# GpSimd normalises the head outputs of a delta-rule attention stage; head weights folded into the projection, GpSimd's reset moved to the iteration's end

## The chip, the cores and the metric

The kernel runs on one core of a Trainium2 chip. The metric is the device time of one execution in microseconds (us), from the start of the program to its end. Besides its DMA queues the core has TensorE (PE; its weight loads are shown as PEld), VectorE (DVE), ScalarE (ACT), GpSimd (POOL) and SyncE (SP, which here only issues transfers). Each engine works through its own instructions in order; semaphores order them against each other.

## What is computed

Six blocks work on x of 64 x 64 tokens x 128 channels in float32, each added to x: self-attention, cross-attention, a routed feed-forward layer, a gated delta-rule attention with spiking gates, a gated cross-attention, and a second routed layer. The change lies in the fourth block alone:

```python
h = silu(conv(rms(x)));  q, k, v, drive = h @ Wq, h @ Wk, h @ Wv, h @ Wspike     # 8 heads of 64
alpha_base = silu(h @ Wau + bau) @ Wad + bad;  beta_base = h @ Wbeta + bbeta
# per time step (spike: the membrane 0.9 * mem + drive is over its threshold)
alpha = sigmoid(alpha_base + alpha_spike * spike)
beta  = sigmoid(beta_base + sum(spike * beta_spike, -1))
active = sum(spike) > 0                            # per head; inactive: alpha = 1, beta = 0
s = s * alpha;  s = s + (beta * k) * (v - k @ s);  out = q @ s
# after the steps
y = out * rsqrt(mean(out * out) + 1e-6) * head_norm_w
y = x + (y @ Wo) * sigmoid(gate);  z = rms(y) * ff_norm_w
y = y + (silu(z @ Wff1) * (z @ Wff3)) @ Wff2
```

## The kernel before

The block is the function `delta()`. The time recurrence is not stepped: for each group of 8 sequences (512 tokens, `T`) the triangular system of 64 steps is inverted by doubling. There are 8 groups (`NG`), and the loop over `it` from -2 to 8 is a software pipeline written out by hand on each engine. In iteration `it` the core work is that of group `it`, the front work (projections, norms, decays, beta) that of group `it + 1`, and the tail work (head norm, output projection, feed-forward) that of group `it - 1`. Heads go in four pairs, `hp` or `j` from 0 to 3. Iterations 1 to 6 have core, front and tail; iteration 0 has no tail, 7 no front, 8 only a tail.

The core work runs over stages. TensorE forms the products of a head pair (`diag`, L2231; `products(g, l)`, L2244) in two pairs of PSUM banks; VectorE takes them over into `AP` with `masked(g, stage, hp)` (L2708 for stage 0, L2719 for the rest) and multiplies k and q by the decays (`scale_first`, L2727; `scale`, L2742 and L2744); GpSimd multiplies `kr` and the decays in its own `scale` (L2630, L2631). The products of pair `hp` at a level may only overwrite a bank pair when the `masked` two before it is done (`pair_free`). `first_inverse` (VectorE L2750 and L2753, four pairs) builds the first inverse; `ax` and `xw` (L2259, L2268, L2290) double it level by level, ScalarE copying their PSUM banks out (`w_out` L2476, `x_out` L2482 and L2484). `ax(it, 1)` needs `first_inverse` and all of `masked(it, 2, ...)`. The first step of a core writes the negative identity into half of `AP`: `reset` on GpSimd (L2619), which waits until the last `ax` of the group before has read it.

The products of front and tail work go through two further PSUM banks (6 and 7) in turn, in an order given by the list `FILLS`: a fill may only start when what the fill two before it wrote has been read. For the change the order ..., k 0 to 3, cb, wo, q 0 to 3, al 0 to 3, ... counts: q 0 waits for the reading of cb, q 1 for that of wo.

The tail norm: ScalarE squares a head pair's output, TensorE sums (`t_ss`, L2178 and L2150), ScalarE makes Ln and Exp of it (`t_rms`, L2450 and L2452; the third and fourth wait until the first and second `o_normed` have read the double buffer), VectorE multiplies output, half the head weight and this reciprocal norm (`o_normed`, L2773, four times), TensorE projects (`t_wo`, L2188), VectorE multiplies by the gate (`t_gated`, L2782).

The count of spikes and the beta logits (`f_cb`): TensorE L2164 and L2166 in the bank of cb; ScalarE copies the logits (L2508); VectorE then turns the counts into 1e30 where a head had no spike, else 0 (L2839, rows 64 to 95 of `au`), which goes as an extra input row with a weight of one into the decays' product (`f_al`, L2138). Sigmoid of beta is ScalarE's `f_beta` (L2531), the masking by `active` VectorE's (L2844); the product `f_kr` (L2150) of TensorE needs it.

VectorE's order in an iteration: `masked(0)` with `scale_first`, four times; `o_normed` four times; `masked(1)` and `scale(0)` of pairs 0 and 1; `f_cb`; the same of pairs 2 and 3; `t_gated`; `first_inverse` four times; `masked(2)` and `scale(1)` four times; `t_y`; and on. Late in the iteration it advances the membrane of group `it + 2` in small steps on 128x32 elements (L2767, L2769), between which `f_beta`, `f_kr` and `t_out` stand. GpSimd's order: `reset`, `z_tok` (L2655), `scale(0)`, `squares` of k (L2648), `scale(1)`, `residual`, `scale(2)`, `squares` of q, `scale(3)`, `scale(4)`, and, after a wait for the end of the membrane, `spikes` (L2635).

## Time and profile before

| | us |
|---|---|
| median of 3 runs | 2898.83 (lowest 2896.13) |
| the profiled execution | 2903.73 |
| its span, first to last instruction | 2901.9 |
| `delta()` in the span | about 1095 to 2398 |
| one full iteration | about 156 to 160 |
| granted TensorE clock, mean over the span | 0.829 of full |
| busy: PE, DVE, ACT, POOL | 2361.8, 1634.3, 969.8, 732.5 |

One of the three runs took 7392.36 us; the median is not touched by it. A timeline row gives start, duration, engine, line, operation, output from input, count, and in brackets how long the engine was idle before it and what released it.

### The profile page before, as it was taken

The page shows a single profiled execution, that of the slowest core. Times are in us where ns is not written, and L with a number is a line of the kernel's source. Part 1 is how long each engine was busy: PE and PEld are TensorE (multiplying, and loading weights), DVE is VectorE, ACT ScalarE, POOL GpSimd, SP SyncE. Part 2 cuts the span into 40 slices and gives each one's busy share as a digit, 9 for nine tenths or more (in the row PEclk, how much of TensorE's full clock was granted, in tenths as well). Part 3 has the DMA queues.
Part 4 walks back from the last instruction along what each step waited for, and adds up shares of the span by engine and source line. Part 5 has one row for each costly group of instructions (what it writes and reads, how often), then busy time and mean ns, then how long its engine had stood idle before and what let it go on. Part 6 is the DMA issues. An engine that isn't in the chain of part 4 may idle for free. (4 is left out here: it accounts for less than half of the span.)

```text
span 2901.9 us, 74066 instructions
## 1 busy us (share of the span) xinstructions
PE 2361.8 (81%) x31128; PEld 1655.3 (57%) x31167; DVE 1634.3 (56%) x4406; ACT 969.8 (33%) x1910; POOL 732.5 (25%) x852
## 2 busy tenths in 40 slices
PE   7898989998778576888989898989988886956674
PEld 4666666666665332555656564656656755745553
DVE  4455555545362474767676676767564713477334
ACT  3343343434212253342424343333434331310222
POOL 0110101101016452424231314232241300112663
PEclk9799898979559786999999998999998975555776
DMA  4000000000021131000000000000000002000114
GB/s 150 9 1 9 9 9 5 1 1 1 7 74 44 47 135 47 3 21 6 21 6 21 6 3 24 3 20 6 2 6 2 7 1 90 2 30 19 44 44 113
DMA packets 42507, 75.80 MB, mean 26 GB/s; under 512 B 5989, under 2 KB 27245, under 8 KB 39621
## 3 DMA queue, kind: packets, MB, share of 16 engines
q1 hardware_dynamic: 35140, 56.63, 5.7%
q0 software_dynamic: 7040, 14.43, 1.8%
q8 instruction: 252, 4.13, 0.6%
q14 instruction: 75, 0.61, 0.1%
HBM read 46.73 MB, written 24.31 MB: 24 GB/s over the span
## 5 line engine op out<-in xcount | busy, mean ns | idle before, releaser
L2630 POOL TENSOR_TENSOR delta_scaled_beta_k<-delta_scaled_beta_k,delta_decays 128x256 f32<-128x256 f32 x160 | 122.1, 763 | 434.0 <-DVE weights_sb L2742 225.2
L2719 DVE COPY_PREDICATED delta_neg_a_and_p_t<-delta_level_int,bank 128x256 f32<-128x256 uint8 x384 | 179.2, 537 | 74.1 <-PE bank L2244 73.2
L2244 PE MATMUL bank<-weights_sb,delta_scaled_beta_k 64*64 64x64 f32 x6144 | 136.1, 234 | 85.6 <-DVE delta_neg_a_and_p_t L2719 79.2
L2268 PEld LDWEIGHTS bank<-delta_inverse,delta_neg_a_and_p_t 64*64 64x64 f32 x5120 | 176.8, 145 | 46.2 <-issue 45.8
L2268 PE MATMUL bank<-delta_inverse,delta_neg_a_and_p_t 64*64 64x64 f32 x5120 | 199.7, 232 | 0.0
L2244 PEld LDWEIGHTS bank<-weights_sb,delta_scaled_beta_k 64*64 64x64 f32 x6144 | 116.0, 145 | 122.6 <-DVE delta_neg_a_and_p_t L2719 98.1
L683 POOL TENSOR_TENSOR attn_probs<-attn_probs,attn_row_sum 128x512 f32<-128x512 f32 x64 | 65.4, 1043 | 397.7 <-DVE attn_row_sum L766 397.7
L2476 ACT ACTIVATE delta_two_less_ax<-bank 128x512 f32<-128x512 f32 x160 | 94.8, 597 | 208.6 <-PE bank L2268 208.4
L303 PE MATMUL bank<-attn_z_self_t,weights_sb 128*128 128x256 f32 x512 | 153.4, 452 | 13.3 <-DVE attn_cross_values L741 9.6
L312 PE MATMUL bank<-attn_w_value_out,attn_z_self_t 128*64 128x512 f32 x512 | 143.0, 684 | 2.1 <-DVE attn_z_value_out L706 1.4
L2150 PE MATMUL bank<-delta_head_rows,norm_sel 16*128 16x512 f32 x192 | 117.6, 712 | 27.2 <-DVE delta_head_rows L2844 19.8
L2290 PE MATMUL bank<-delta_two_less_ax,delta_inverse_t 64*64 64x64 f32 x4096 | 133.9, 219 | 2.4 <-issue 2.3
L750 DVE TENSOR_REDUCE attn_row_max<-bank 128x8 f32<-128x512 f32 x128 | 82.5, 686 | 90.9 <-PE bank L392 61.3
L303 PEld LDWEIGHTS bank<-attn_z_self_t,weights_sb 128*128 128x128 f32 x512 | 107.7, 223 | 45.1 <-issue 20.4
L2290 PEld LDWEIGHTS bank<-delta_two_less_ax,delta_inverse_t 64*64 64x64 f32 x4096 | 127.6, 136 | 3.5 <-issue 3.5
L2482 ACT ACTIVATE delta_inverse<-bank 128x512 f32<-128x512 f32 x128 | 76.4, 597 | 134.8 <-PE bank L2290 134.8
L574 ACT ACTIVATE attn_z_value_out<-bank 128x512 f32<-128x512 f32 x96 | 57.0, 594 | 166.1 <-PE bank L312 166.1
L2648 POOL TENSOR_TENSOR delta_kq_squared<-weights_sb 128x512 f32<-128x512 f32 x64 | 73.5, 1179 | 121.3 <-PE bank L2145 113.2
L2744 DVE TENSOR_TENSOR weights_sb<-weights_sb,delta_decays 128x512 f32<-128x512 f32 x128 | 97.9, 765 | 0.0
L2465 ACT ACTIVATE weights_sb<-bank 128x512 f32<-128x512 f32 x64 | 38.1, 597 | 178.2 <-PE bank L2131 178.2
L1392 POOL DMA_INDIRECT moe_z_sorted<-z_rows,moe_take_row x71 | 69.0, 971 | 112.7 <-DVE moe_take_row L1684 91.3
L1543 ACT ACTIVATE moe_hidden<-moe_pre_gelu 128x256 f32<-128x256 f32 x71 | 29.6, 417 | 198.2 <-DVE moe_pre_gelu L1705 121.1
(535 smaller groups left out, 5325.8 us busy)
## 6 DMA issues: line engine op xcount, KB each, us to landing
delta_drives<-front_drive SPq DMA_DIRECT2D x7, 1024.0 KB, 3.9
weights_sb<-in_w_moe_dram SPq DMA_DIRECT2D x1, 4352.0 KB, 14.7
z_rows<-moe_z_all SPq DMA_DIRECT2D x16, 256.0 KB, 2.3
delta_odd_spikes<-delta_drives SPq DMA_DIRECT2D x4, 1024.0 KB, 5.0
weights_sb<-moe_outs SPq DMA_DIRECT2D x8, 512.0 KB, 7.2
weights_sb<-delta_drives SPq DMA_DIRECT2D x3, 1024.0 KB, 5.1
weights_sb<-in_w_delta_dram SPq DMA_DIRECT2D x1, 2816.0 KB, 9.8
weights_sb<-in_ctx_tok_dram SPq DMA_DIRECT2D x8, 264.0 KB, 5.9
```

The lines of the kernel that those rows point to most:

```text
L303: last = pe.matmul(out_[:, i * 256:(i + 1) * 256], wA[:, 0 if kind == "q" else 1, m * 128:(m + 1) * 128], zA[:, g % 2, :], start=True, sto ...
L312: last = pe.matmul(out_[64 * hh:64 * hh + 64, :], zA[:, g % 2, 64 * b:64 * b + 64], vo[:, hh, 512 * half:512 * half + 512], start=True, st ...
L750: dve.tensor_reduce(mx[:, o % 2, h, :], ps[h], AX, ALU.max).then_inc(s["max"], 1)
L2150: return pe.matmul(out_[:, :], nsel[r, j, :], hrows[r, :], start=start, stop=True)
L2244: last = pe.matmul(two[eo][rows(sg), b4 * 64:b4 * 64 + 64], kr[r, hp, t], second(kq[r, g % 2, :, hp, t], c), start=b < 2, stop=True, skip_ ...
L2268: last = pe.matmul(out_[rows(sg), u], AP[rows(sg), hp, eo, b4, 0, :], X[rows(sg), hp, u], start=False, stop=True, skip_group_check=True)
L2290: last = pe.matmul(out_[rows(sg), u], lhsT, rhs, start=b == 0, stop=True, skip_group_check=True)
L2476: act.activation(W[:, hp, :], bank[4 + hp % 2][:, :], ACT.Copy).then_inc(s["w"], 1)
L2482: act.activation(X[:, hp, :], bank[4 + hp % 2][:, :], ACT.Copy).then_inc(s["x"], 1)
L2630: pool.tensor_tensor(r_[:, :, 0, :], r_[:, :, 0, :], a_[:, :, 1, 0:1].to_broadcast([128, T // (2 * c), c]), ALU.mult)
L2719: last = dve.copy_predicated(second(AP[:, hp, eo, :, :, :].rearrange("p b i n -> p (b i) n"), c), m_, PAIR[hp % 2][eo][:, :].rearrange("p ...
L2744: dve.tensor_tensor(v, v, f.unsqueeze(1).to_broadcast([128, 2, m, c]), ALU.mult).then_inc(s["scaled_kq"], 1)
```

## The change

VectorE's `o_normed` goes to GpSimd as a plain product of two tensors, at the start of GpSimd's iteration; the half head weight is multiplied once into the four blocks of the output projection's weights. VectorE's `f_cb` goes to ScalarE as Relu(1 - count), right behind the copy of the logits; the 1e30 goes into the weight row. GpSimd's `reset` and `z_tok` go from the start of an iteration to the end of the one before, ahead of `spikes`. ScalarE's `f_beta` goes ahead of `w_out(it, 5)`. On VectorE `first_inverse` goes ahead of `t_gated`.

```diff
@@ ScalarE, f_cb(g)
                         act.activation(hrows[BETA, :], J[at_fill["cb", g, 0] % 2][96:128, :], ACT.Copy).then_inc(s["logit"], 1)
+                        if g >= 1:
+                            act.wait_ge(s["al_ps"], nth_of("al", g - 1, 3))
+                            act.wait_ge(s["beta"], g)
+                        act.activation(au[64:96, :], J[at_fill["cb", g, 0] % 2][64:96, :], ACT.Relu, bias=ones[64:96, :], scale=-1.0)\
+                            .then_inc(s["cb_rd"], 1)
@@ ScalarE, iteration
                         act.preload_act_table(ACT.Sigmoid)
+                        if front:
+                            f_beta(it + 1)
                         if core:
                             w_out(it, 5)
                         if front:
-                            f_beta(it + 1)
                             f_alpha(it + 1)
@@ GpSimd
+                    def o_normed(g, j):
+                        pool.wait_ge(s["o_rstd"], HDP * g + j + 1)
+                        pool.tensor_tensor(oT[:, j, :], oT[:, j, :], orstd[:, j % 2, :], ALU.mult).then_inc(s["o_normed"], 1)
@@ GpSimd, iteration
-                        if core:
-                            reset(it)
                         if tail:
-                            z_tok(it - 1)
+                            for j in range(HDP):
+                                o_normed(it - 1, j)
                         if core:
                             scale(it, 0)
...
                             scale(it, 3)
                             scale(it, 4)
+                        if front:
+                            reset(it + 1)
+                        if core:
+                            z_tok(it)
                             if it + 2 < NG:
                                 spikes(it + 2)
@@ VectorE
-                    def o_normed(g, j):
-                        dve.wait_ge(s["o_rstd"], HDP * g + j + 1)
-                        dve.scalar_tensor_tensor(oT[:, j, :], oT[:, j, :], half_w[:, j:j + 1], orstd[:, j % 2, :], ALU.mult, ALU.mult)\
-                            .then_inc(s["o_normed"], 1)
...
-                    def f_cb(g):
-                        dve.wait_ge(s["logit"], g + 1)
-                        if g >= 1:
-                            dve.wait_ge(s["al_ps"], nth_of("al", g - 1, 3))
-                        dve.tensor_scalar(au[64:96, :], J[at_fill["cb", g, 0] % 2][64:96, :], 0.0, 1e30, ALU.is_equal, ALU.mult)\
-                            .then_inc(s["cb_rd"], 1)
-
                     def f_beta(g):
                         dve.wait_ge(s["sigmoid"], g + 1)
+                        dve.wait_ge(s["cb_rd"], g + 1)
@@ VectorE, once
-                    dve.tensor_scalar(half_w[:, :], col("headw", 0, HDP), 0.5, None, ALU.mult)
+                    link(dve.tensor_scalar(half_w[:, :], col("headw", 0, HDP), 0.5, None, ALU.mult))
+                    for n in range(HDP):
+                        w_ = wD[:, 7, n * 128:(n + 1) * 128]
+                        dve.tensor_scalar(w_, w_, half_w[:, n:n + 1], None, ALU.mult)
...
-                    dve.tensor_copy(wD[64:72, 4, :], nsel[0:8, 0:HDP, :].rearrange("p j d -> p (j d)"))
+                    dve.tensor_scalar(wD[64:72, 4, :], nsel[0:8, 0:HDP, :].rearrange("p j d -> p (j d)"), 1e30, None, ALU.mult)
+                    dve.memset(ones[:, :], 1.0)
@@ VectorE, iteration
-                        if tail:
-                            for j in range(HDP):
-                                o_normed(it - 1, j)
-                        if core:
-                            for hp in (0, 1):
+                        if core:
+                            for hp in range(HDP):
                                 masked(it, 1, hp)
                                 scale(it, 0, hp)
-                        if front:
-                            f_cb(it + 1)
-                        if core:
-                            for hp in (2, 3):
-                                masked(it, 1, hp)
-                                scale(it, 0, hp)
+                            for hp in range(HDP):
+                                first_inverse(it, hp)
                         if tail:
                             t_gated(it - 1)
                         if core:
-                            for hp in range(HDP):
-                                first_inverse(it, hp)
                             for hp in range(HDP):
                                 masked(it, 2, hp)
```

## Rows read from the trace of the kernel before

**Rows 1.** Busy time by stretch: length, PE, PEld, DVE, ACT, POOL, PEclk, DMA, GB/s
```profile
1100.00:2420.00 1320.00, 1133.09 (x21273) 749.80 (x21274) 832.64 (x2031) 472.88 (x797) 358.99 (x445) 0.90 0.04 14
```

**Rows 2.** Waits in 1105 to 2420: total us, times, longest us
```profile
DVE a_alpha_hidden_and_empty L2839 <- ACT delta_head_rows L2508: 68.3, 8, 10.5
```

**Rows 3.** Waits of PE in one full iteration, 1600 to 1757
```profile
PE bank L2244 <- DVE delta_neg_a_and_p_t L2719: 9.6, 4, 6.6
```

**Rows 4.** Timeline of the same iteration, 1611 to 1628
```profile
1611.36 1.41 DVE L2773 SCALAR_TENSOR_TENSOR delta_two_less_ax<-delta_two_less_ax,delta_half_head_norm,delta_o_rstd 128x512 f32<-128x512 f32 x2
...
1612.30 1.16 PE L2244 MATMUL bank<-weights_sb,delta_scaled_beta_k 64*64 64x64 f32 x64
...
1615.31 1.28 DVE L2719 COPY_PREDICATED delta_neg_a_and_p_t<-delta_level_int,bank 128x256 f32<-128x256 uint8 x2
...
1619.12 3.53 PE L2131 MATMUL bank<-group_conv_out,weights_sb 128*128 128x512 f32 x4
...
1627.13 3.84 PE L2188 MATMUL bank<-weights_sb,delta_two_less_ax 128*128 128x128 f32 x32
...
1627.86 0.69 DVE L2839 TENSOR_SCALAR a_alpha_hidden_and_empty<-bank 32x512 f32<-32x512 f32 x1 [8.64 <-ACT delta_head_rows L2508]
```

**Rows 5.** Timeline of the same iteration, 1632 to 1649
```profile
1632.34 1.98 PE L2131 MATMUL bank<-group_conv_out,weights_sb 128*128 128x512 f32 x4
...
1633.05 1.02 DVE L2750 TENSOR_TENSOR delta_inverse_t<-delta_neg_a_and_p_t,delta_two_eye 128x512 f32<-128x512 f32 x1
...
1639.65 1.26 DVE L2719 COPY_PREDICATED delta_neg_a_and_p_t<-delta_level_int,bank 128x256 f32<-128x256 uint8 x2
...
1640.96 1.13 PE L2244 MATMUL bank<-weights_sb,delta_scaled_beta_k 64*64 64x64 f32 x32 [6.64 <-DVE delta_neg_a_and_p_t L2719]
...
1643.77 3.15 PE L2131 MATMUL bank<-group_conv_out,weights_sb 128*128 128x512 f32 x4
...
1648.57 0.38 PE L2259 MATMUL bank<-delta_two_eye_bf,ident_bf 128*128 128x512 bf16 x1
```

**Rows 6.** Timeline of the same iteration, last inverse level, 1730 to 1735
```profile
1730.70 0.72 ACT L2531 ACTIVATE delta_head_rows<-delta_head_rows,delta_beta_bias 32x512 f32<-32x512 f32 x1
1731.44 2.56 ACT L2525 ACTIVATE delta_decays<-delta_decays,small_sb 128x512 f32<-128x512 f32 x4
...
1732.28 1.09 PE L2150 MATMUL bank<-delta_head_rows,norm_sel 16*128 16x512 f32 x2 [2.25 <-DVE delta_head_rows L2844]
...
1734.50 0.60 ACT L2484 ACTIVATE delta_inverse_t<-bank 128x512 f32<-128x512 f32 x1 [0.50 <-PE bank L2290]
```

**Rows 7.** Single lines: duration ns min/median/max, first and last start
```profile
L2648 POOL TENSOR_TENSOR delta_kq_squared<-weights_sb x64: 1034/1041/1486, 1108.3 to 2152.5; 128x512 f32<-128x512 f32 x64
L2619 POOL COPY delta_neg_a_and_p_t<-delta_neg_eye x8: 1887/1892/1893, 1128.0 to 2201.3; 128x2048 f32<-128x2048 f32 x8
L2655 POOL TENSOR_SCALAR weights_sb<-x_all,group_x_moments,group_x_rstd x32: 788/797/1226, 1289.7 to 2307.5; 128x128 f32<-128x128 f32 x32
L2742 DVE TENSOR_TENSOR weights_sb<-weights_sb,delta_decays x32: 716/946/1106, 1159.5 to 2250.0; 128x512 f32<-128x512 f32 x32
```

**Rows 8.** Timeline: membrane steps beside GpSimd's squares; VectorE's slack at `f_kr`
```profile
1597.32 0.69 DVE L2850 SCALAR_TENSOR_TENSOR delta_scaled_beta_k<-weights_sb,bank 128x512 f32<-128x512 f32 x1 [5.43 <-PE bank L2150]
...
1676.67 4.04 POOL L2648 TENSOR_TENSOR delta_kq_squared<-weights_sb 128x512 f32<-128x512 f32 x4 [14.75 <-PE bank L2145]
...
1678.81 0.96 DVE L2769 SCALAR_TENSOR_TENSOR delta_membrane<-delta_odd_spikes 128x32 f32<-128x32 f32 x1
...
1688.48 0.23 DVE L2769 SCALAR_TENSOR_TENSOR delta_membrane<-delta_odd_spikes 128x32 f32<-128x32 f32 x1
```

**Rows 9.** Timeline of setup, of iteration 0 and of iteration 7
```profile
1101.70 0.59 PE L2332 MATMUL bank<-delta_beta_bias,delta_count_and_beta_w 128*32 128x1 f32 x8 [32.52 <-DVE delta_count_and_beta_w L2864]
...
1182.17 1.14 PE L2244 MATMUL bank<-weights_sb,delta_scaled_beta_k 64*64 64x64 f32 x32 [3.44 <-DVE delta_neg_a_and_p_t L2719]
...
2259.73 1.14 PE L2244 MATMUL bank<-weights_sb,delta_scaled_beta_k 64*64 64x64 f32 x32 [6.17 <-DVE delta_neg_a_and_p_t L2719]
```

More of the change, by code:

```diff
@@ L2052, in body @@
                 log_eps = sb("log_64_eps", [128, 1], ctx=ctx)
+                ones = sb("one", [128, 1], ctx=ctx)
                 zzT = sb("z_out_t", [128, T], ctx=ctx)
```

## The prediction, made before the changed kernel was run

> **What bounds the kernel now.** I read the page first, then the busy time by stretch, then the waits, then the timeline of one full iteration (number 3), and last single lines. The change touches nothing outside `delta()`. There the reader is to see that TensorE is busy 1133 of 1320 us, VectorE 833, at a granted clock of 0.90 [rows 1]. So TensorE sets the pace, and a microsecond is gained only where TensorE waits or runs at its lower clock, and only if what releases it comes earlier.
>
> The waits name one place. VectorE stands at `f_cb` 8 times for 68.3 us in all, released by ScalarE's copy of the logits [rows 2]. That alone costs nothing: TensorE is meanwhile at k, cb and wo. But behind `f_cb` in VectorE's order stand two pairs of `masked(1)`/`scale(0)`, `first_inverse` and `masked(2)`, and TensorE waits for them afterwards: 9.6 us in one iteration on L2719 alone, 6.6 us of it in one piece [rows 3].
>
> The timeline shows how. VectorE does `o_normed` from 1611.36, and `masked(1)` can only start at 1615.31, though its products began at 1612.30 with 0.58 us a pair [rows 4]. It waits 8.64 us, until 1627.86, for the cb product that TensorE's order puts behind k [rows 4]. `first_inverse` then runs 1633.05 to 1639.65, and the product that needs the `masked(2)` behind it starts at 1640.96, after 6.64 us idle [rows 5]. `ax(1)` starts at 1648.57 [rows 5]. Around these waits TensorE is at its lower level for a while: four k instructions take 3.53 us, and four q instructions once 3.15, where the same shape took 1.98 at 1632.34 [rows 4, 5].
>
> **The change, part by part (iteration 3, then times its count).**
>
> *`f_cb` off VectorE, `o_normed` off VectorE, `first_inverse` ahead of `t_gated`.* These three have one answer. The first pair's products end at about 1612.9, so `masked(1)` starts at about 1613.0. From its old start at 1615.31 to the beginning of the wait at 1619.2 (1627.86 less 8.64) two pairs take 3.9 us [rows 4]; four take 7.8. `first_inverse` takes 6.6 [rows 5]. VectorE is through at 1613.0 + 7.8 + 6.6 = 1627.4.
> TensorE: its short waits at 1613 to 1619 (the 9.6 less the 6.64, less about 0.6 at the end) go, and with them the slow k, so `t_wo` ends not at 1627.13 + 3.84 = 1631.0 but about 4 earlier, near 1627. `t_gated` follows at once (about 0.7), so `masked(2)` starts near 1628.1; the product that came 1.3 behind it (1639.65 to 1640.96 [rows 5]) could start at 1629.4, but TensorE is at q until about 1630.0. Against 1640.96 that is 11.0 us. If the second q pair runs at full clock, 1.2 more (3.15 less 1.98), so 12.2 at `ax(1)`. What comes behind `ax(1)` has the same order on every engine and shifts as a whole.
>
> *`o_normed` on GpSimd.* Four times 1.04 us, the price of a 128x512 product there [rows 7], against 1.41 for two on VectorE [rows 4]. ScalarE's reciprocal norms come one by one until about 1613.7 (the third no longer waits for VectorE), so GpSimd ends near 1614.9. `t_wo` wants it at about 1623: 8 us of cover. GpSimd's `scale(0)` wants the engine when VectorE's first `scale(0)` is done, at about 1614.8: no cover, no loss. If the cover were gone, each us would cost one.
> The price is contention. Beside GpSimd, VectorE's two-input products take up to 1.106 instead of 0.716 us [rows 7], and its small membrane steps 0.96 instead of 0.23 [rows 8], about one for each GpSimd instruction of 1.01. Here `scale_first` of pairs 2 and 3 has 1 to 1.5 us of slack, since VectorE is at `masked(1)` before its products are; the first `scale(0)` has none. I take 0.8 us lost; bounds 0 and 2.1 (two GpSimd instructions of 1.04). The Trainium skill, "SBUF — State Buffer", "Who interferes with whom", speaks against this part: a VectorE instruction with two SBUF inputs and a GpSimd instruction that reads SBUF exclude each other for a whole instruction. The membrane rows agree with it. By it the loss would be at most one GpSimd instruction per VectorE instruction that meets one, which is the upper bound just taken from the rows.
>
> *`f_cb` on ScalarE.* One instruction of about 0.7 us behind the logit copy, in place of 0.69 on VectorE [rows 4] behind the same copy. q 0 is released at the same distance. ScalarE has nothing queued behind it but the q copies, which wait for TensorE. Bound above: should Relu need a table load, that is hidden in the same gap, as TensorE still has `t_wo` of 3.84 us and products to do. No trace row shows Relu; the Trainium skill, "ScalarE: Activation LUTs", "Table sets", says that cheap functions, relu among them, are in every set, so by it there is no load. Its new waits (for the decays' product and beta of the group before) are over long before.
>
> *`f_beta` ahead of `w_out(5)`.* TensorE waited 2.25 us at `f_kr(0)` until 1732.28 [rows 6]. Sigmoid now comes first, 0.72 us [rows 6], and delays `w_out(5)` and `ax(5)` by about that; then TensorE gains 1.5. But `f_alpha`, 2.56 us, still stands ahead of `x_out(5)` and would end near 1734.0, and that copy came at 1734.50 [rows 6]. So 0.5; bounds 0 and 1.5.
>
> *`reset` and `z_tok` at the end.* 1.89 and 4 x 0.80 us, 5.1 together [rows 7], from about 1730 (the last `ax` read) beside the membrane. At one membrane step per GpSimd instruction or blocked entirely, VectorE loses 4 to 5. It started 4 us earlier, as masking beta no longer waits for `w_out(5)` (it ran behind 1730.70 + 0.72 [rows 6], now near 1728), and `f_kr(1)` later waited 5.43 us for TensorE [rows 8]. Cost zero; if both covers were gone, up to 5. What comes free at the start of the iteration was idle time. `spikes` comes as before, behind the membrane.
>
> *Per full iteration*: 12.2 - 0.8 + 0.5 = 11.9, of which 1.2 hangs on the clock; I take 11.5. Bounds: 8 (contention at its bound, nothing from the clock, one wait of 1 us left) and 14 (all slow stretches at full clock). Six of them: 69 (48 to 84).
>
> *Iteration 0* (no tail): `masked(1)` to `first_inverse` without the wait would end near 1172; the product of 1182.17 [rows 9] could start near 1174: 8 (6 to 9). *Iteration 7* (no front, so no `f_cb`): `o_normed` goes (2.3) and the wait for `t_wo` ahead of `first_inverse` (1.4): 3.7 (2 to 6), its gap of 6.17 [rows 9] shrinks but stays. *Iteration 8*: the last `o_normed` is on the path, 1.04 for 0.70: -0.3. *Setup*: four weight products of 128x128 and a link ahead of L2332, for which TensorE waits [rows 9]: -1 (0 to -2.9, four times the 0.72 of a product four times as large [rows 7]).
>
> Sum: 69 + 8 + 3.7 - 0.3 - 1 = 79.4. The profiled execution took 2903.7, so 2824; its span is 1.8 shorter, and it lies 4.9 above the median of 2898.8. Against the median I predict **2820**. With the bounds (53 to 98): 2801 to 2846.
>
> **Rivals.**
> *The wait moves.* `t_gated` stands now between `first_inverse` and `masked(2)`; if `t_wo` comes late (k still slow, its fills waiting), VectorE waits there and TensorE gets only what `o_normed` cost, 2.8 to 4 an iteration: about 24 in all, 2875. Against it: VectorE's 1627.4 falls together with `t_wo`'s end, so a late `t_wo` costs one for one and would have to be 8 us late.
> *Contention takes the gain.* `scale_first`, `scale(0)` and the membrane are each held, and the membrane's end makes `f_kr` late: 2.1 + 2 an iteration beyond mine, 6 times: 25, so 2845 to 2850. For it: 0.96 instead of 0.23 [rows 8]. Against it: 5.43 us of slack.
> *Slower: the clock.* k ran at nearly half speed though TensorE's waits ahead of it were short [rows 4]. If the whole stretch 1612 to 1635, about 20 us of matmul at full speed, ran at the lower level (3.53 for 1.98, so times 1.8), it would cost 16 and leave the 10 of waits: -6 an iteration, about 2940. It decides from some 12 us of slow stretch on. Against it: the slow pieces lie behind waits, and those go.
> *It does nothing* to TensorE, as the stalls hide under it: refuted for most by the 9.6 us [rows 3]; it is in the first rival.
>
> **How the numbers follow.** Forecast 0.70, contention 0.13, the wait moves 0.10, clock 0.05, more gain than my bounds 0.02. About 2% (58 us, below 2841 or above 2957) is what a measurement of this kernel can tell. Faster: the forecast but for its upper edge, and a third of contention: 0.74. Same: 0.22. Slower: 0.04. The range 2797 to 2860 takes in the forecast's bounds and contention.
>
> **What would show it.** In the profile after: no wait of VectorE before L2719 on ScalarE's logit copy; TensorE's waits on L2719 down from 9.6 to some 1 to 2 an iteration; full iterations of 144 to 147 us; GpSimd's `o_normed` near 1.04 us each; PEclk above 0.90 in the stage. Waits of VectorE at `t_gated` over 3 us, or of TensorE at `t_wo` on GpSimd, or a k product still at 3.5 us, would prove it wrong.

## The result: 3.5% faster, 102 us at the median

The changed kernel took 2795.24 us (median of 4 runs, 2787.47 to 2803.7) against 2897.48 us for the kernel before on the same chip: ratio 0.9654, 95% interval 0.9616 to 0.9691. The prediction was 2820, range 2797 to 2860, against a median before of 2898.83; on that base the ratio gives 2798.5, which is just inside the range, while the bare median of 2795.24 lies 1.8 us below its lower edge. The direction and the mechanism held; the gain was some 30% larger than forecast (102 us, not 79), because TensorE's clock gave back more than it was booked with. It is also above the forecast's own bounds of 53 to 98 us: the case that the prediction gave a chance of 0.02.

| us | before | after |
|---|---|---|
| profiled execution | 2903.73 | 2794.32 |
| its span | 2901.9 | 2792.5 |
| span ahead of `delta()`'s first setup matmul | 1101.7 | 1089.1 |
| iterations 0 to 6 (first product to first product) | 1078.6 | 981.9 |
| of it iteration 0 | 140.7 | 130.2 |
| iterations 1 to 6, each | 154.3 to 158.8 | 138.7 to 143.7 |
| granted TensorE clock over the span | 0.829 | 0.850 |
| busy: PE, DVE, ACT, POOL | 2361.8, 1634.3, 969.8, 732.5 | 2307.4, 1623.0, 977.2, 781.7 |

By its first products, a full iteration of the kernel before is 154.3 to 158.8 us, a little less than the 156 to 160 named at the start.

The first thing to take off is what isn't the change. Of the 109.4 us between the two spans, 12.6 lie ahead of `delta()`, where both kernels do the same work; 2.7 are lost behind it. `delta()` itself went from 1296.2 to 1196.7 us: 99.5 us. That is what the sum of the prediction has to be held against, and from here on the text speaks of it.

The stretch of [rows 1] once more, moved to where the changed kernel does the same work (length, PE, PEld, DVE, ACT, POOL, PEclk, DMA, GB/s):

```profile
1087.00:2308.00 1221.00, 1094.61 (x21274) 723.82 (x21275) 821.86 (x1993) 478.86 (x805) 408.99 (x476) 0.93 0.05 15
```

TensorE runs the same number of matmuls (21274, before 21273) in 99 us less, and the 99 has two parts: its idle time fell from 1320.0 - 1133.1 = 186.9 to 1221.0 - 1094.6 = 126.4, that is 60.5, and its busy time fell by 38.5, at a granted clock of 0.93 instead of 0.90. So two fifths of the gain are not waiting that went, but the same instructions run faster. Of iterations 0 to 6, TensorE's busy time fell by 28.4 us in the stretches from `products(0)` to `ax(1)` and by 7.3 from `ax(5)` to the end of the iteration; the stretches between gave nothing.

The waits of TensorE in the changed kernel, 1560 to 1720, which is iteration 3 (1554.0 to 1694.5) less its first products and with the beginning of iteration 4 (total us, times, longest):

```profile
PE bank L2260 <- ACT delta_two_less_ax L2477: 3.3, 2, 2.7
PE bank L2245 <- DVE delta_neg_a_and_p_t L2733: 3.2, 5, 0.8
```

L2733 is what was L2719, L2245 what was L2244. The 6.6 us of one piece in [rows 3] are gone; what is left there comes in pieces of at most 0.8, and within iteration 3 alone it is 2.4 us in four pieces. The wait on ScalarE (L2477) is of later stages: its 2.7 us were there before, 0.6 at `ax(5)` are new. Over the whole program the page's group of these products says it again, idle time before them 28.8 us, where it was 85.6:

```profile
L2245 PE MATMUL bank<-weights_sb,delta_scaled_beta_k 64*64 64x64 f32 x6144 | 126.4, 225 | 28.8 <-DVE delta_neg_a_and_p_t L2733 22.0
```

The timeline of iteration 3, the counterpart of [rows 4, 5] (start, duration, engine, line, operation, idle before it and its releaser):

```profile
1565.30 1.17 PE L2245 MATMUL bank<-weights_sb,delta_scaled_beta_k 64*64 64x64 f32 x64
...
1566.06 1.31 DVE L2733 COPY_PREDICATED delta_neg_a_and_p_t<-delta_level_int,bank 128x256 f32<-128x256 uint8 x2 [1.21 <-PE bank L2245]
...
1567.18 1.39 DVE L2756 TENSOR_TENSOR weights_sb<-weights_sb,delta_decays 128x512 f32<-128x512 f32 x1
...
1569.86 0.70 PE L2245 MATMUL bank<-weights_sb,delta_scaled_beta_k 64*64 64x64 f32 x32 [0.84 <-DVE delta_neg_a_and_p_t L2733]
...
1570.48 1.98 PE L2132 MATMUL bank<-group_conv_out,weights_sb 128*128 128x512 f32 x4
...
1574.83 0.68 DVE L2764 TENSOR_TENSOR delta_inverse_t<-delta_neg_a_and_p_t,delta_two_eye 128x512 f32<-128x512 f32 x1
...
1576.95 3.84 PE L2189 MATMUL bank<-weights_sb,delta_two_less_ax 128*128 128x128 f32 x32
...
1577.67 0.68 ACT L2513 ACTIVATE a_alpha_hidden_and_empty<-bank,delta_one 32x512 f32<-32x512 f32 x1
...
1580.97 0.65 DVE L2791 SCALAR_TENSOR_TENSOR weights_sb<-delta_gate,bank 128x512 f32<-128x512 f32 x1
1581.54 1.29 DVE L2733 COPY_PREDICATED delta_neg_a_and_p_t<-delta_level_int,bank 128x256 f32<-128x256 uint8 x2
...
1583.73 0.71 PE L2245 MATMUL bank<-weights_sb,delta_scaled_beta_k 64*64 64x64 f32 x32
...
1584.65 0.70 PE L2245 MATMUL bank<-weights_sb,delta_scaled_beta_k 64*64 64x64 f32 x32 [0.21 <-DVE delta_neg_a_and_p_t L2733]
...
1588.92 0.38 PE L2260 MATMUL bank<-delta_two_eye_bf,ident_bf 128*128 128x512 bf16 x1
```

The reader is to see four things. `masked(1)` starts 0.76 us behind the start of its products (before 3.01). VectorE comes without a wait from `masked(1)` to `first_inverse` (1574.83), and finds `t_wo` just finished for `t_gated` (L2791, no bracket, so no wait). The k product beside it takes 1.98 us, not 3.53. And `ax(1)`, the row at 1588.92, comes 23.62 us behind the products' start, where it was 36.27.

The same stretch by engine, before and after (columns as in [rows 1]), shows why it stops at 23.6:

```profile
1612.30:1648.60 36.30, 26.62 (x320) 14.40 (x319) 26.33 (x42) 7.55 (x13) 16.48 (x20) 0.86 0.00 1
```
```profile
1565.30:1588.90 23.60, 22.54 (x319) 12.50 (x319) 22.70 (x33) 7.30 (x12) 17.13 (x20) 1.00 0.01 2
```

TensorE is now busy 22.54 of 23.60 us at its full level of 2.4 GHz (granted clock 1.00), where it was busy 26.62 of 36.30 at 0.86. The stretch is 23.6 us in every one of iterations 1 to 6 (before 34.9 to 38.2). It is at TensorE's own length but for 1.06 us; nothing on VectorE or GpSimd can shorten it by more than that.

The end of the iteration, the counterpart of [rows 6]:

```profile
1666.18 0.72 ACT L2537 ACTIVATE delta_head_rows<-delta_head_rows,delta_beta_bias 32x512 f32<-32x512 f32 x1
...
1667.58 0.39 PE L2260 MATMUL bank<-delta_two_eye_bf,ident_bf 128*128 128x512 bf16 x1 [0.63 <-ACT delta_two_less_ax L2477]
...
1670.37 1.12 PE L2151 MATMUL bank<-delta_head_rows,norm_sel 16*128 16x512 f32 x2
...
1670.53 1.92 POOL L2626 COPY delta_neg_a_and_p_t<-delta_neg_eye 128x2048 f32<-128x2048 f32 x1 [29.09 <-PE bank L2269]
1670.72 1.80 DVE L2781 SCALAR_TENSOR_TENSOR delta_odd_spikes<-delta_membrane,delta_odd_spikes 128x32 f32<-128x32 f32 x1
...
1672.44 3.37 POOL L2666 TENSOR_SCALAR weights_sb<-x_all,group_x_moments,group_x_rstd 128x128 f32<-128x128 f32 x4
1672.56 0.23 DVE L2783 SCALAR_TENSOR_TENSOR delta_membrane<-delta_odd_spikes 128x32 f32<-128x32 f32 x1
...
1674.22 2.08 PE L2291 MATMUL bank<-delta_inverse_t,delta_two_less_ax 64*64 64x64 f32 x64 [0.71 <-ACT delta_inverse_t L2485]
```

`f_kr(0)` (L2151) no longer waits 2.25 us. In its place stand 0.63 at `ax(5)`, since Sigmoid goes ahead of `w_out(5)`, and 0.71 in the middle of `xw(5)`, since `f_alpha` still holds up `x_out(5)`. `reset` (L2626) comes with one membrane step of 1.80 us instead of some 0.2; beside `z_tok` (L2666) they stay at 0.22 to 0.27.

GpSimd's `o_normed` on the page:

```profile
L2659 POOL TENSOR_TENSOR delta_two_less_ax<-delta_two_less_ax,delta_o_rstd 128x512 f32<-128x512 f32 x32 | 48.7, 1521 | 157.2 <-ACT delta_o_rstd L2453 157.2
```

It takes 1.52 us on average, not the 1.04 of [rows 7].

### The profile page after: what moved, and what is told of

Same layout as the page of the kernel before. It is cut to its first block and busy times, and to the rows that moved or that the text cites. A ratio compares the mean times of both kernels' runs of the same rounds, so it can differ in the third digit from the quotient of the medians.

```text
span 2792.5 us, 74079 instructions
## 1 busy us (share of the span) xinstructions
PE 2307.4 (83%) x31128; PEld 1616.3 (58%) x31167; DVE 1623.0 (58%) x4371; ACT 977.2 (35%) x1918; POOL 781.7 (28%) x884
## 5 line engine op out<-in xcount | busy, mean ns | idle before, releaser
L2733 DVE COPY_PREDICATED delta_neg_a_and_p_t<-delta_level_int,bank 128x256 f32<-128x256 uint8 x384 | 179.5, 538 | 70.4 <-PE bank L2245 69.8
L2477 ACT ACTIVATE delta_two_less_ax<-bank 128x512 f32<-128x512 f32 x160 | 94.3, 598 | 205.1 <-PE bank L2269 204.8
L303 PE MATMUL bank<-attn_z_self_t,weights_sb 128*128 128x256 f32 x512 | 147.1, 437 | 14.8 <-DVE attn_cross_values L741 11.1
L2245 PE MATMUL bank<-weights_sb,delta_scaled_beta_k 64*64 64x64 f32 x6144 | 126.4, 225 | 28.8 <-DVE delta_neg_a_and_p_t L2733 22.0
L2245 PEld LDWEIGHTS bank<-weights_sb,delta_scaled_beta_k 64*64 64x64 f32 x6144 | 108.0, 137 | 63.6 <-issue 32.0
L2151 PE MATMUL bank<-delta_head_rows,norm_sel 16*128 16x512 f32 x192 | 119.2, 722 | 10.7 <-DVE delta_kq_squared L2820 3.8
L2659 POOL TENSOR_TENSOR delta_two_less_ax<-delta_two_less_ax,delta_o_rstd 128x512 f32<-128x512 f32 x32 | 48.7, 1521 | 157.2 <-ACT delta_o_rstd L2453 157.2
```

The source lines that it names most:

```text
L303: last = pe.matmul(out_[:, i * 256:(i + 1) * 256], wA[:, 0 if kind == "q" else 1, m * 128:(m + 1) * 128], zA[:, g % 2, :], start=True, sto ...
L2151: return pe.matmul(out_[:, :], nsel[r, j, :], hrows[r, :], start=start, stop=True)
L2245: last = pe.matmul(two[eo][rows(sg), b4 * 64:b4 * 64 + 64], kr[r, hp, t], second(kq[r, g % 2, :, hp, t], c), start=b < 2, stop=True, skip_ ...
L2477: act.activation(W[:, hp, :], bank[4 + hp % 2][:, :], ACT.Copy).then_inc(s["w"], 1)
L2733: last = dve.copy_predicated(second(AP[:, hp, eo, :, :, :].rearrange("p b i n -> p (b i) n"), c), m_, PAIR[hp % 2][eo][:, :].rearrange("p ...
```

## Experiments

The theory: the gain comes from VectorE reaching `first_inverse` and `masked(2)` without a wait; it takes `f_cb` off VectorE and the new order together, for with one alone the wait moves; the clock rises because TensorE's gaps go. The rivals: the wait at `f_cb` was only a place where VectorE stood, and `o_normed` or the order brought the gain; or the end of the iteration (`f_beta`, `reset`, `z_tok`) did.

In the first group of four, the kernel before itself took 2839.8 us; in the others it took 2896 to 2899. So medians are compared as ratios within a group, and across groups the length of iterations 0 to 6 is used (each group ran on a chip of its own; in the first one the traces are some 50 us shorter outside these iterations): 1078.6 before, 981.9 after and 981.4 in a second profile of the changed kernel, so it repeats to about 1 us. The changed kernel didn't run in the first group; its ratio of 0.9654 from its own group, set against theirs, gives 57, 17, 26 and 50 us for u_cb, u_on, u_beta and u_inv, and the iterations give 61, 21, 26 and 44.

### u_cb: the changed kernel with the count back on VectorE

```diff
@@ VectorE, iteration
-                            for hp in range(HDP):
+                            for hp in (0, 1):
                                 masked(it, 1, hp)
                                 scale(it, 0, hp)
+                        if front:
+                            f_cb(it + 1)
...
+                            for hp in (2, 3):
+                                masked(it, 1, hp)
+                                scale(it, 0, hp)
@@ ScalarE, f_cb: Relu removed; f_cb as before on VectorE, the weight row 1 again
```

> The changed kernel with the spike count's step f_cb back on VectorE, between the second and third pair of masked(1), and no Relu; all else as changed. Theory (the stall at f_cb, with two pairs and first_inverse queued behind it, made the loss): VectorE waits some 8 us an iteration for the logit copy again, TensorE about 7 to 9 us on the products behind it; 7 iterations, so 55 to 70 us slower than the changed kernel, about 2855. Rival (taking o_normed off VectorE made the gain, f_cb was hidden under TensorE's k, cb and wo): at most 15 us slower, about 2805.

Measured: ratio 0.9855 (0.9819 to 0.9892). Iterations 0 to 6 take 1043.1, 61 us more than the changed kernel. The waits in iteration 3 (VectorE, then TensorE):

```profile
DVE a_alpha_hidden_and_empty L2842 <- ACT delta_head_rows L2508: 7.0, 1, 7.0
```
```profile
PE bank L2131 <- DVE weights_sb L2785: 5.8, 1, 5.8
```

VectorE waits at `f_cb` again, and TensorE now pays behind `t_gated` (L2785): q 1 needs the bank that `t_gated` reads, and that stands behind all of `first_inverse`. So `f_cb` is worth 61 of the 97 us when all else is in place. The other way round, all the other edits together bring 36 us with `f_cb` still on VectorE.

### u_on: the changed kernel with `o_normed` back on VectorE, the weights not folded

```diff
-                        pool.tensor_tensor(oT[:, j, :], oT[:, j, :], orstd[:, j % 2, :], ALU.mult).then_inc(s["o_normed"], 1)
+                        dve.scalar_tensor_tensor(oT[:, j, :], oT[:, j, :], half_w[:, j:j + 1], orstd[:, j % 2, :], ALU.mult, ALU.mult)\
+                            .then_inc(s["o_normed"], 1)
@@ VectorE, iteration: o_normed four times again behind masked(0)
```

> The changed kernel with o_normed back on VectorE ahead of masked(1), the head weights not folded; all else as changed. Theory (f_cb is the cause): masked(1) starts 2.5 to 3 us later, VectorE has about 1 us of slack at the end of first_inverse, 0.8 us of contention goes: 1 to 2 us an iteration, so 7 to 15 us slower than the changed kernel, about 2806. Rival (o_normed is the cause): 4 us an iteration and the lower clock behind it, 30 to 50 us slower, about 2835.

Measured: ratio 0.9715 (0.9676 to 0.9755), iterations 0 to 6 at 1002.6, 20.7 more, all of it in the six iterations with a tail. From the products to `ax(1)` it takes 25.2 to 28.1 us instead of 23.6, on average 2.8 more. That is about what VectorE's four instructions take (1.41 for two in [rows 4], 0.75 for each of the others); I had expected half of it.

### u_beta: the changed kernel with `f_beta` behind `w_out(it, 5)`

```diff
                         act.preload_act_table(ACT.Sigmoid)
-                        if front:
-                            f_beta(it + 1)
                         if core:
                             w_out(it, 5)
                         if front:
+                            f_beta(it + 1)
                             f_alpha(it + 1)
```

> The changed kernel with ScalarE's f_beta back behind w_out(5). Theory of the prediction (f_alpha limits it): 0.5 us an iteration, 4 us slower in all, about 2799. Rival (TensorE's wait of 2.25 us also lowers its clock in the work behind it, which the iteration read for the prediction showed least): 1.5 to 2.5 us an iteration, 10 to 17 us slower, about 2808.

Measured: ratio 0.9747 (0.9707 to 0.9788), iterations 0 to 6 at 1008.4, 26.5 more. That is 3.8 an iteration, where the prediction had put the edit at 0.5. Iteration 3, timeline:

```profile
1668.54 1.89 POOL L2625 COPY delta_neg_a_and_p_t<-delta_neg_eye 128x2048 f32<-128x2048 f32 x1 [30.06 <-PE bank L2269]
1669.88 1.09 DVE L2846 SCALAR_TENSOR_TENSOR delta_head_rows<-a_alpha_hidden_and_empty,delta_head_rows 32x512 f32<-32x512 f32 x1 [7.30 <-ACT delta_head_rows L2537]
1671.12 1.09 PE L2151 MATMUL bank<-delta_head_rows,norm_sel 16*128 16x512 f32 x2 [2.66 <-DVE delta_head_rows L2846]
1672.14 5.50 PE L2291 MATMUL bank<-delta_inverse_t,delta_two_less_ax 64*64 64x64 f32 x128
```

Two things besides the wait. The moved `reset` stretches the masking of beta (L2846) from 0.68 to 1.09. And `xw(5)`, behind the wait, takes 5.50 us, where it takes 3.95 at the full clock: 1.55 us go with the lower level. So there were two candidates for what the prediction missed, the clock and `reset`; the run u_beta_reset below separates them.

### u_inv: the changed kernel with `t_gated` ahead of `first_inverse`

```diff
-                            for hp in range(HDP):
-                                first_inverse(it, hp)
                         if tail:
                             t_gated(it - 1)
+                        if core:
+                            for hp in range(HDP):
+                                first_inverse(it, hp)
```

> The changed kernel with t_gated back ahead of first_inverse. Theory: VectorE reaches t_gated some 6 us before TensorE has ended t_wo, waits there, and first_inverse (6 to 6.6 us) comes after: 5 to 6 us an iteration and the clock behind the gap, 35 to 45 us slower than the changed kernel, about 2835: the stall of f_cb would for the most part have moved here. Rival (first_inverse is covered wherever it stands): no difference, 2795.

Measured: ratio 0.983 (0.9796 to 0.9864), iterations 0 to 6 at 1026.2, 44 more. The waits from 1560 to 1720, VectorE, then TensorE:

```profile
DVE weights_sb L2791 <- PE bank L2189: 5.9, 1, 5.9
```
```profile
PE bank L2245 <- DVE delta_neg_a_and_p_t L2733: 6.7, 4, 4.2
```

The wait has moved from `f_cb` to `t_gated`, as expected: the change of order is worth 44.

### after_again and u_reset: the changed kernel again, and with `reset` and `z_tok` back at the start

```diff
@@ GpSimd, iteration
+                        if core:
+                            reset(it)
                         if tail:
+                            z_tok(it - 1)
                             for j in range(HDP):
                                 o_normed(it - 1, j)
...
-                        if front:
-                            reset(it + 1)
-                        if core:
-                            z_tok(it)
```

> The changed kernel as it is, as the measure for the other kernels on this chip. Ratio to the kernel before 0.965, 8 full pipeline iterations (0 to 6, up to the start of the core of iteration 7) in about 982 us of its trace.

> The changed kernel with GpSimd's reset and z_tok back at the start of the iteration, ahead of o_normed. Theory: they fit into the 10 us between spikes and the first reciprocal norm, so nothing is lost there, and the membrane steps are freed of them; as TensorE does not wait for the membrane, within 3 us of the changed kernel. Rival (their move is part of the gain): 2 to 5 us an iteration slower, 15 to 30 us. Rival (they hold the membrane and f_kr in the changed kernel): 5 to 15 us faster.

Measured: 0.9642 (0.9621 to 0.9662) and 0.9642 (0.9614 to 0.967); iterations 0 to 6 at 981.4 and 978.8. With `f_beta` early, the place of `reset` and `z_tok` makes no difference that could be told from one profile each. At the start they fit into GpSimd's idle time: ahead of the first `o_normed` of an iteration it is some 10.4 us in the changed kernel and 5.4 in u_reset, and `o_normed` starts equally early in both. At the end the membrane's slack takes them. With a late `f_beta` it is otherwise, see u_beta_reset.

### o_cb: the kernel before with the count on ScalarE, and nothing else

The diff is the first hunk of the change and `f_cb` removed from VectorE's order.

> The kernel before with one part of the change alone: f_cb on ScalarE, masked(1) of all four pairs in a row; t_gated stays ahead of first_inverse, o_normed on VectorE. Theory (each part only pays together: the wait at f_cb moves to t_gated): VectorE reaches t_gated early and waits for t_wo, first_inverse comes after, as when the order alone was undone (31.2 us from the first products to ax(1), against 23.6 with all parts and 36.4 before); about 5 us an iteration, 35 to 45 us faster than before, ratio 0.985 to 0.988. Rival (f_cb alone is the cause): 60 us or more, ratio below 0.979.

Measured: ratio 0.9933 (0.9914 to 0.9953), iterations 0 to 6 at 1061.6, so 17 us less than before. The waits of VectorE and TensorE in iteration 3:

```profile
DVE weights_sb L2788 <- PE bank L2189: 7.3, 1, 7.3
```
```profile
PE bank L2245 <- DVE delta_neg_a_and_p_t L2725: 7.6, 4, 4.3
```

The wait of 8.64 us [rows 4] stands as 7.3 at `t_gated`. So the prediction's first rival, the wait that moves, is what `f_cb` does without the new order.

### o_cb_inv: the kernel before with the count on ScalarE and `first_inverse` ahead of `t_gated`

```diff
-                            for hp in (0, 1):
+                            for hp in range(HDP):
                                 masked(it, 1, hp)
                                 scale(it, 0, hp)
-                        if front:
-                            f_cb(it + 1)
...
+                            for hp in range(HDP):
+                                first_inverse(it, hp)
                         if tail:
                             t_gated(it - 1)
@@ and the first hunk of the change
```

> The kernel before with two parts of the change: f_cb on ScalarE and first_inverse ahead of t_gated. o_normed stays on VectorE, f_beta, reset and z_tok where they were. Theory (these two together take first_inverse out from behind a wait for TensorE; o_normed is worth 3 us, f_beta 2): from the first products to ax(1) 26 to 28 us an iteration instead of 36.4, the last part as before at 31 to 34; iterations 0 to 6 in about 1015 us (1078.6 before, 982 with all), ratio to before about 0.978. Rival (the parts add up one by one, f_cb 17 us as measured, the order 45): 62 us, also near 0.978 in time, but with 30 us or more from the first products to ax(1).

Measured: ratio 0.9754 (0.972 to 0.9789), 2825.69 against 2898.69, so 73 of 102 us. Iterations 0 to 6 take 1019.4, 59 less than before: 42 more than `f_cb` alone brings. (The rival gives nearly the same time; what speaks against it is the stretch, which it put at 30 us or more.) The stretch from the products to `ax(1)` is 26.7 or 26.8 us in all of iterations 0 to 6, in the full ones 3.1 above the changed kernel's 23.6: VectorE still has the four `o_normed`, which u_on priced at 2.8. The order alone, with `f_cb` left on VectorE in the kernel before, was not run.

### o_on: the kernel before with `o_normed` on GpSimd, the folded weights and the moved `reset` and `z_tok`

> The kernel before with the other part alone: o_normed on GpSimd with the folded weights, reset and z_tok at the end of the iteration; f_cb stays on VectorE. Theory: VectorE reaches f_cb 2.5 us earlier and waits there longer; TensorE's short waits of the first pairs go (some 2 us), the 6.6 us behind f_cb stay, and reset, which begins with the last ax, holds VectorE's masking of beta for 0.4 us and so f_kr(0): 0 to 2 us an iteration, ratio 0.995 to 1.0. Rival (less work on VectorE is what pays): 3.5 us an iteration and more, ratio below 0.991.

Measured: 0.9977 (0.9952 to 1.0001), iterations 0 to 6 at 1077.6 against 1078.6. Waits in full iteration 3, VectorE then TensorE:

```profile
DVE a_alpha_hidden_and_empty L2841 <- ACT delta_head_rows L2508: 7.5, 1, 7.5
```
```profile
PE bank L2244 <- DVE delta_neg_a_and_p_t L2726: 7.2, 2, 6.6
PE bank L2259 <- ACT delta_two_less_ax L2476: 2.7, 1, 2.7
PE bank L2150 <- DVE delta_head_rows L2846: 2.7, 1, 2.7
```

The 6.6 us piece of [rows 3] is untouched. Counted from the start of the products, VectorE is at `f_cb` 1.5 us earlier, and TensorE is through cb 2.7 us earlier; so VectorE's wait is 7.5 us and not longer, as expected, but shorter than the 8.64 before. Products to `ax(1)` fall from a mean of 36.4 to 33.8, and `ax(5)` to the end rises from 32.5 to 34.1, where the moved `reset` meets the masking of beta (wait at L2150 2.7, was 2.25). So the run holds two things against each other: `o_normed` brings 2.6 an iteration in its own stretch, nearly the 2.8 that it is worth in the changed kernel, and the moved `reset` beside a late `f_beta` takes 1.6 of it back at the end (another 0.6 goes between `ax(1)` and `ax(5)`, untraced). `o_normed` on GpSimd with `reset` left at the start was not run.

### u_beta_reset: the changed kernel with `f_beta` back, and `reset` and `z_tok` back too

> The changed kernel with ScalarE's f_beta back behind w_out(5) and GpSimd's reset and z_tok back at the start of the iteration. Undoing f_beta alone took the last part, from ax(5) to the next core, from 30.5 to 33.1 or 34.4 us. Theory (reset starts when the last ax is read and holds VectorE's masking of beta, 1.09 instead of 0.68 us, so TensorE waits 2.7 instead of 2.3 us): 32 to 33 us, as in the kernel before. Rival (it is TensorE's lower clock behind the wait for beta, whatever GpSimd does): 33 to 34.4 us as without the reset's move undone, and xw(5) at the lower clock.

Measured: ratio 0.9688 (0.9643 to 0.9732), iterations 0 to 6 at 995.5, 13.6 more than the changed kernel, against 26.5 for u_beta. Iteration 3, timeline:

```profile
1676.39 1.09 PE L2151 MATMUL bank<-delta_head_rows,norm_sel 16*128 16x512 f32 x2 [2.25 <-DVE delta_head_rows L2846]
1677.41 5.50 PE L2291 MATMUL bank<-delta_inverse_t,delta_two_less_ax 64*64 64x64 f32 x128
```

The masking of beta is back at 0.68 us and the wait at 2.25, but `xw(5)` still takes 5.50. So a slow `xw(5)` doesn't need `reset`. But `reset` has a share: behind a wait of 2.66 us `xw(5)` took 5.49 to 5.93 in all 18 iterations of the runs that have one (all of u_beta and o_on, the last of before, o_cb, o_cb_inv and u_beta_reset), behind one of 2.25 it came at 3.95 in five of 24. The stretch from `ax(5)` to the iteration's end:

| iterations 1 to 6, us | ax(5) to end | mean |
|---|---|---|
| before | 31.1, 32.7, 31.1, 32.7, 34.2, 33.1 | 32.5 |
| u_beta_reset | 31.1, 34.1, 32.7, 32.7, 32.7, 34.2 | 32.9 |
| u_beta | 33.1, 34.4, 33.1, 33.1, 34.4, 33.1 | 33.5 |
| changed | 30.5, 30.5, 30.5, 30.8, 30.5, 29.8 | 30.4 |

So the change is worth 2.1 here against before, and `reset` beside a late `f_beta` costs some 0.6, in iteration 0 3.5. The two runs lie 12.9 us apart over iterations 0 to 6: 7.1 of it are in this stretch, 5.5 between `ax(1)` and `ax(5)`, where no cause was traced and two profiles of the changed kernel differ by 2.3. Of u_beta's 26.5 us, 22.8 lie in this stretch. Both expectations were half right: the mean of 32.9 is where the theory put it, the slow `xw(5)` is what the rival said.

### imp1 and imp2: further along the same road

The changed kernel's largest wait in a full iteration is 2.7 us at `ax(3)`, until ScalarE has done the norms and a table load:

```profile
1625.49 1.28 ACT L2586 ACT_TABLE_LOAD   x1
...
1627.44 0.39 PE L2260 MATMUL bank<-delta_two_eye_bf,ident_bf 128*128 128x512 bf16 x1 [2.71 <-ACT delta_two_less_ax L2477]
```

```diff
@@ ScalarE, both kernels: two of w_out(3)'s copies between the steps of the norms, the table load behind w_out(3)
                         link(act.activation(r_[both, :], r_[both, :], ACT.Ln, bias=eps_tiles[RMS_EPS][both, :]))
                         if g >= 1:
+                            w_out(g - 1, 3, (0,))
...
-                        act.preload_act_table(ACT.Silu)
                         if core:
-                            w_out(it, 3)
+                            w_out(it, 3, (2, 3) if front else range(HDP))
+                        act.preload_act_table(ACT.Silu)
@@ ScalarE, both: x_out(5) ahead of f_alpha
+                        if core:
+                            x_out(it, 5)
                         if front:
                             f_alpha(it + 1)
@@ TensorE, imp1 only: the norms' product in two halves, one ahead of products(3)
@@ VectorE, imp2 only: seven membrane steps ahead of masked(4)
```

> The changed kernel with three further moves: TensorE sums the squares of k right after ax(2), so that GpSimd squares q beside level 2 and TensorE does not stand in f_nrm (some 3 us an iteration); ScalarE does the first two w_out(3) between the steps of f_nrm and loads the Silu table after w_out(3) (TensorE's wait of 2.7 us on L2477); f_alpha behind x_out(5) (0.7 us). Theory: 5 to 6 us an iteration, 7 iterations, 35 to 45 us faster than the changed kernel, ratio to before about 0.950. Rival (GpSimd's squares beside VectorE's two-input products of level 3 hold these up, and the gain comes back as waits on L2733): less than 15 us.

> The changed kernel with ScalarE's first two w_out(3) between the steps of f_nrm and the Silu table loaded after w_out(3) (TensorE's wait of 2.7 us on L2477), f_alpha behind x_out(5) (0.7 us), and seven membrane steps ahead of masked(4), where VectorE waits 3.8 us for TensorE, so that they do not stand ahead of masked(5). The f_nrm of the run before stays whole: split, it took 7.2 us of TensorE instead of 6.3. Theory: 3 to 4 us an iteration, 20 to 28 us faster than the changed kernel, ratio to before about 0.956. Rival (the gain comes back as TensorE's waits on masked(5), 4.2 us in the run before): less than 10 us.

Measured: imp1 0.960 (0.9575 to 0.9625) beside the changed kernel's 0.9642 in the same group, iterations 0 to 6 at 968.4; imp2 0.9546 (0.9498 to 0.9594), iterations 0 to 6 at 949.3. `ax(5)` to the end falls from 30.5 to 29.5 in both; in imp2's trace `xw(5)` runs through in one piece of 3.95 us. In imp1 the first half of the norms' product stands ahead of `products(3)`: VectorE waits 7.5 us at `masked(4)`, and TensorE then 2.9 us for `masked(5)`:

```profile
PE bank L2245 <- DVE delta_neg_a_and_p_t L2741: 4.4, 5, 2.9
```

In imp2 TensorE waits in an iteration for no more than 1.1 us at a time, and at L2260 only this is left of 3.3:

```profile
PE bank L2260 <- ACT delta_two_less_ax L2477: 0.6, 1, 0.6
```

imp2 takes 2766.4 us where before takes 2898.7, some 28 us less than the changed kernel by the ratios. Of its three edits, the one at `ax(5)` is told apart by its 1.0 an iteration; how the rest splits between ScalarE's order and the membrane steps was not tried.

## Why the prediction came out as it did

**Right: the place and the mechanism.** VectorE's wait at `f_cb` and what stands behind it is the bulk of the gain: 61 us go when `f_cb` returns, 44 when the order returns. The signs named for the profile came in the main: no wait on the logit copy ahead of L2719's counterpart, the products' waits in iteration 3 down from 9.6 to 2.4 (said 1 to 2), PEclk up, k at 1.98. Two did not: `o_normed` is not near 1.04 us, and a full iteration is shorter than said.

**Right: the parts have one answer.** `f_cb` alone brought 17, `o_normed` with the moved `reset` and `z_tok` 1, `f_cb` with the order 59, all of it 97. Undone one at a time from the full change they cost 61, 21, 44 and 26, together 152, which is more than the whole. A price per edit doesn't exist here; the prediction was right to price the three at once.

**Mis-sized: the stretch up to `ax(1)`, 11.4 forecast, 12.8 measured.** The working was 11.0 for the path through VectorE, less 0.8 for contention, plus 1.2 for q's clock. In iteration 3 its parts can be held against the rows. From the start of the products to the product that stood behind the 6.64 us, the time fell from 28.66 (1640.96 less 1612.30) to 18.43 us (1583.73 less 1565.30): 10.2, which is the 11.0 less the 0.8. The path was another, though. TensorE doesn't wait there any more; it came late by the 0.84 us that it waited at 1569.86 for `masked(1)` of the second pair, as the first of VectorE's products took 1.39 us, beside the last `o_normed`, where it was 0.72 before. VectorE's four pairs took 8.8 us and not 7.8 (1566.06 to 1574.83); what they lost behind that wait ran beside TensorE's k, cb and `t_wo`. From that product to `ax(1)` the time fell from 7.61 to 5.19 us: 2.4, where 1.2 was booked. The term that was too small is this one, the clock behind the wait. The prediction priced it for q alone (1.17), but the two products ahead of q were slow too, 1.13 us each against 0.71 and 0.70 after, and a wait between them went from 0.62 to 0.21. The row of the kernel before that shows it:

```profile
1642.71 1.13 PE L2244 MATMUL bank<-weights_sb,delta_scaled_beta_k 64*64 64x64 f32 x32 [0.62 <-DVE delta_neg_a_and_p_t L2719]
```

Full iterations came at 138.7 to 143.7 us, below the 144 to 147 that the prediction named as its sign.

**Mis-sized: `f_beta`, 0.5 forecast, 2.1 measured.** The step that failed: I read the end of the iteration in number 3 alone. There the wait of 2.25 us is followed by `xw(5)` at 3.95 us:

```profile
1733.30 3.95 PE L2290 MATMUL bank<-delta_inverse_t,delta_two_less_ax 64*64 64x64 f32 x128
```

Four of the six full iterations of the kernel before look like this one instead (iteration 2):

```profile
1576.22 1.09 PE L2150 MATMUL bank<-delta_head_rows,norm_sel 16*128 16x512 f32 x2 [2.25 <-DVE delta_head_rows L2844]
1577.24 5.50 PE L2290 MATMUL bank<-delta_inverse_t,delta_two_less_ax 64*64 64x64 f32 x128
```

Against the two iterations at 31.1 the changed kernel's mean of 30.4 is a gain of 0.7, close to what was forecast; the other 1.4 is the mean of what runs at the lower level behind the wait: 1.55 in `xw(5)` in four of six, and some more in iterations 5 and 6. The clock part was in the trace, one iteration away from where I looked.

**The clock as a whole.** The prediction had 1.2 an iteration for it by name, and the slow k inside its 11.0 (3.53 less 1.98). Together that is 2.7 an iteration, about 16 for six. Measured were 38.5 us less busy time for the same matmuls over the stretch. Less than half of it had been booked. The 20 us that are missing in the forecast are about this difference: of waits it had some 63 us, and 60.5 us of idle time went. The slower-clock rival went the other way altogether: with the gaps much of the lower level went.

**Right for a wrong reason: `reset` and `z_tok` at nothing.** I took 4 to 5 us as held from the membrane and covered by slack. `z_tok` holds no step (0.22 to 0.27 beside it), `reset` one, by 1.6. What the prediction didn't see is that the move isn't free with a late `f_beta` (u_beta against u_beta_reset, 12.9 us); the early `f_beta` of the same change covers it. The Trainium skill, "SBUF — State Buffer", "Who interferes with whom", has it that a VectorE instruction with two SBUF inputs and a GpSimd instruction that reads SBUF contend. The trace agrees for `reset` (a step of 1.80), for the squares [rows 8] and for `o_normed` (1.39 and 1.64 us of VectorE beside it), and disagrees for `z_tok`'s TENSOR_SCALAR (0.22 to 0.27), where the measurement decides.

**Right: Relu without a load.** It follows the logit copy directly in 0.68 us with no table load between them (1577.67), as the Trainium skill, "ScalarE: Activation LUTs", "Table sets", has it of cheap functions.

**The sum, once more.** Forecast against measured: six full iterations 69 against 86.2 (14.4 each, of it 12.8 and 2.1, less 0.5 at the levels between); iteration 0 8 against 10.5; iterations 7 and 8 3.4 against 3.1; setup -1 against -0.3. Together 79.4 against 99.5. The upper bound given for a full iteration was 14, "all slow stretches at full clock"; what came is that case, and 0.4 more. The likeliest value should have stood closer to it: the prediction argued itself that the slow pieces lie behind waits which go, and then counted one of them.

## What to carry to other kernels

When an engine waits in the middle of its order, list all that stands behind the wait and each next wait of the same engine; taking one away alone moves the wait to the next (17 us), taking both brings the gain (59). Price waits of TensorE together with the matmuls behind them, and read those in every iteration, not in one: the same instruction at 3.95 and at 5.50 us is a term of the sum. Compute the length of the next engine in line for the stretch (here TensorE's 22.5 us): it caps the gain and covers much of the contention, but not where that engine itself still waits (0.84 us). And when a run joins two edits, look at each one's own stretch before calling one worthless: in o_on 2.6 us an iteration were gained in one and most of it lost in another, and the total showed 1 us.

## What the runs showed of the hardware that I had not expected

Behind TensorE's wait of 2.66 us the 128 matmuls of `xw(5)` took 5.49 to 5.93 us instead of 3.95 in all 18 iterations that have it; behind 2.25 us they took 5.36 to 6.07 in 19 of 24 and 3.95 in five, two of them in the kernel before (iterations 1 and 3). What decides between these no run here shows.

GpSimd's product of two 128x512 tensors took 1.04 us for the squares [rows 7], but at least 1.26 and on average 1.52 as `o_normed`, with some 2.33 for the second of each iteration, which starts together with a VectorE product of 128x1024 with two SBUF inputs. That product took its usual 1.22; the next one, which started before `o_normed` had ended, took 1.64:

```profile
1561.43 1.22 DVE L2741 TENSOR_TENSOR weights_sb<-weights_sb,delta_decays 128x1024 f32<-128x1024 f32 x1
1561.44 2.34 POOL L2659 TENSOR_TENSOR delta_two_less_ax<-delta_two_less_ax,delta_o_rstd 128x512 f32<-128x512 f32 x1 [0.83 <-ACT delta_o_rstd L2453]
...
1563.22 1.64 DVE L2741 TENSOR_TENSOR weights_sb<-weights_sb,delta_decays 128x1024 f32<-128x1024 f32 x1
```

Why the two products differ even where VectorE is idle (1.26 at the least against 1.04) stays open: the squares read one tensor twice and `o_normed` two tensors, but no run changed only that.
